# Routing the last layer's experts: compacted blocks of rows for three batches, dense for the fourth

## The reference, cut to what matters

```python
gate_probs = softmax(xf @ gate_w.T)                     # xf: 1024 tokens x 128
topk_scores, topk_idx = top_k(gate_probs, 2)            # 2 of 8 experts for each token
topk_scores /= sum(topk_scores)
combine = zeros((1024, 8)).at[token, topk_idx].set(topk_scores)
h = relu(einsum('td,ehd->teh', xf, w1) + b1)            # hidden 512, all 8 experts
expert_out = einsum('teh,edh->ted', h, w2) + b2
x = x + einsum('ted,te->td', expert_out, combine)
```

## Time and profile before

| | |
|---|---|
| Median of 3 runs | 380.56 us (379.95 to 383.03) |
| The profiled execution | 382.81 us |
| its span, first to last instruction | 381.0 us |
| PE, DVE, ACT, POOL busy | 314.1, 285.3, 233.0, 131.0 us |
| Mean granted PE clock | 0.900 of full |

### The profile page before, as it was taken

How to read it: one execution, slowest core, us unless ns; L and a number is a source line. 1 busy time by engine, 2 the same in 40 slices (tenths; PEclk the granted TensorE clock), 3 DMA queues, 4 the chain that set the end, 5 groups by cost and what they waited for, 6 DMA issues and landing times.

```text
span 381.0 us, 8587 instructions
## 1 busy us (share of the span) xinstructions
PE 314.1 (82%) x3064; PEld 208.3 (55%) x3064; DVE 285.3 (75%) x741; ACT 233.0 (61%) x380; POOL 131.0 (34%) x209
## 2 busy tenths in 40 slices
PE   0667639997879995797888878878999999999993
PEld 0452314564549974573564545545447676767773
DVE  5687502597987886777968999999997888765663
ACT  1257926776666542323147576756969997768981
POOL 4935897652033451407715032053122203000000
PEclk9999855899999995666558999999989999999999
DMA  7930000000000650000000000000000000010001
GB/s 217 382 150 1 2 0 3 2 2 1 2 2 0 224 223 0 0 3 0 0 2 2 1 2 3 2 3 2 0 2 3 3 2 2 2 29 0 3 3 29
DMA packets 4330, 12.39 MB, mean 33 GB/s; under 512 B 632, under 2 KB 2944, under 8 KB 3264
## 3 DMA queue, kind: packets, MB, share of 16 engines
q1 hardware_dynamic: 4288, 11.84, 8.5%
HBM read 11.31 MB, written 0.52 MB: 31 GB/s over the span
## 4 chain that ended last, share of the span: by engine, by line
PE 28%; DVE 19%; issue 4%; ACT 2%; POOL 0%; DVEq 0%; ACTq 0%; POOLq 0%
PE single L1563 11%; PE double L1550 10%; DVE mx L1053 6%; PE single L1236 2%; PE single L1229 1%; DVE mxc L1040 1%; DVE w L1184 1%; ACT hid L865 1%; DVE xn L933 1%; PE double L1416 1%; DVE y L998 1%; DVE qcn L1063 1%; PE double L1436 1%; DVE sums L992 1%; DVE tmp L1132 1%
## 5 line engine op out<-in xcount | busy, mean ns | idle before, releaser
L788 ACT ACTIVATE region_p<-double 128x1024 f32<-128x1024 f32 x64 | 64.3, 1025 | 23.5 <-PE double L1269 10.8
L688 POOL TENSOR_SCALAR_AFFINE_SELECT region_p<-region_p 128x512 f32<-128x512 f32 (+1 forms) x48 | 39.8, 830 | 58.5 <-ACT region_p L788 57.1
L1202 DVE TENSOR_TENSOR tmp<-hid,tmp 128x1024 f16<-128x1024 f32 x32 | 39.2, 1226 | 20.7 <-ACT tmp L874 20.4
L865 ACT ACTIVATE hid<-double,b1s 128x512 f32<-128x512 f32 x64 | 40.3, 680 | 12.3 <-PE double L1550 10.4
L1563 PE MATMUL single<-w,tmp 128*128 128x128 f16 x768 | 45.5, 219 | 2.2 <-issue 2.2
L1563 PEld LDWEIGHTS single<-w,tmp 128*128 128x128 f16 x768 | 43.9, 98 | 5.6 <-issue 2.9
L1550 PE MATMUL double<-xnT,w 128*128 128x512 f16 x168 | 40.5, 384 | 1.0 <-ACT hid L865 1.0
L646 POOL TENSOR_SCALAR rstd<-mv 128x2 f32<-128x2 f32 x24 | 6.2, 257 | 86.2 <-DVE mv L926 85.5
L874 ACT ACTIVATE tmp<-hid 128x1024 f16<-128x1024 f32 x32 | 33.8, 1057 | 1.6
L1053 DVE TENSOR_REDUCE mx<-double 128x4 f32<-128x1024 f32 (+1 forms) x24 | 29.4, 1225 | 1.5 <-PE double L1436 0.6
L1325 PE MATMUL outs<-region_p,vst 128*32 128x256 f32 x256 | 23.7, 450 | 6.5 <-POOL region_p L688 6.4
(11 more groups left out here) (279 smaller groups left out, 666.3 us busy)
## 6 DMA issues: line engine op xcount, KB each, us to landing
w<-in_w1a SPq DMA_DIRECT2D x2, 1024.0 KB, 11.8
w<-in_w2a SPq DMA_DIRECT2D x2, 1024.0 KB, 13.9
w<-in_w1b SPq DMA_DIRECT2D x2, 1024.0 KB, 4.9
w<-in_w2b SPq DMA_DIRECT2D x2, 1024.0 KB, 7.5
wb<-in_wb SPq DMA_DIRECT2D x1, 837.0 KB, 7.9
row<-in_row SPq DMA_DIRECT2D x1, 800.0 KB, 6.4
x<-in_x SPq DMA_DIRECT2D x4, 128.0 KB, 2.4
out<-x SPq DMA_DIRECT2D x4, 128.0 KB, 1.9
```

Of the source, the lines that this page charges most:

```text
L688: then(g.affine_select(out=v, in_=v, compare_op=ALU.is_ge, fill=0.0, base=0, pattern=[[0, n], [1, P]], channel_multiplier=-1), "prob_masked")
L788: a.activation(probs[:, slot("prob", key), :], psum(step), ACT.Exp, scale=SCALE).then_inc(psum_done[PSUM.slot(step)], 1)
L865: a.activation(hid0[:, slot("hid0", (h, e, n)), cols], psum(step)[:, cols], ACT.Relu, bias=b1s[:, c:c + 1]).then_inc(psum_done[PSUM.slot(s ...
L1202: then(v.tensor_tensor(hid[:, 1].rearrange("p c n -> p (c n)"), hid0[:, slot("hid0", (h, e, n)), :], hid[:, 0].rearrange("p c n -> p (c n) ...
```

## The change

For batches 0, 2 and 1 (`SPARSE`) each token's row is written twice to a buffer `moved` in device memory, at the next free row of each of its two experts. Blocks of 128 rows are then read back, one expert works on a block, and its output is stored over the block's rows. The first 128 rows of each expert are 8 fixed blocks; rows beyond that are 11 blocks whose expert and place come from a table that DVE makes (`tab`) and SP reads into registers. All 19 blocks are always executed. Finally each token's two result rows are fetched and added with their weights. Batch 3 (`LAST`) runs through all 8 experts densely. All products are plain fp32: no splits, no `b1s`, `ws`, `w2s`, `xs`, `hs`. The whole list of steps is a new one, also for work that does not change.

New steps: `rk` (PE counts the tokens of an expert ahead of each token; DVE makes row numbers), `sct` (POOL, 4 indirect writes of 128 rows for each batch), `tab` (10 small DVE operations), `xl` (SP reads a fixed block), `dl` (SP reads two registers, then an expert's weights, 514 KB, and a block), `bt` (transpose), `bu`, `bd` (up, down), `ys` (SP stores a block; for table blocks it reads a register first), `gat` (POOL, 4 indirect reads for each batch), `cb` (DVE sums).

```diff
+SPARSE = (0, 2, 1)
+LAST = 3
+ROOM = T * len(SPARSE)
+OVER = 11
+BLOCKS = NE + OVER
+ROWS = NE * ROOM + (OVER + 1) * P
+        "xl": NE, "wd": 3, "xbT": 2, "yb": 4}
...
 # SP, after the other loads, ahead of w1a and w2a
+            sp.wait_ge(sem("zeros_ready"), 1)
+            sp.dma_start(moved.rearrange("(n p) d -> p n d", p=P),
+                         yb[:, 0, :].unsqueeze(1).to_broadcast([P, ROWS // P, P]))
...
+            for step in ORDER:
+                if kind == "xl":
+                    sp.wait_ge(sem("scattered"), 16 * 4 * len(SPARSE))
+                    sp.dma_start(xl[:, slot("xl", n), :], moved[ROOM * n:ROOM * n + P, :])
+                elif kind == "dl":
+                    sp.wait_ge(sem("scattered"), 16 * 4 * len(SPARSE))
+                    sp.wait_ge(sem("table_ready"), 1)
+                    for b in range(NB):
+                        written(sp, ("ml", b, 3))
+                    read_by_tensor(sp, "xl", n)
+                    read_by_tensor(sp, "wd", n)
+                    of = sp.value_load(table[0:1, 1, i:i + 1], min_val=0, max_val=(NE - 1) * P)
+                    at = sp.value_load(table[0:1, 0, i:i + 1], min_val=0, max_val=ROWS - P)
+                    sp.dma_start(wd[:, slot("wd", n), :], d["experts"][bass.ds(of, P), :])
+                    sp.dma_start(xl[:, slot("xl", n), :], moved[bass.ds(at, P), :])
+                elif kind == "ys":
+                    written(sp, ("bd", n))
+                    if n < NE:
+                        dst = moved[ROOM * n:ROOM * n + P, :]
+                    else:
+                        at = sp.value_load(table[0:1, 0, n - NE:n - NE + 1], min_val=0, max_val=ROWS - P)
+                        dst = moved[bass.ds(at, P), :]
+                    sp.dma_start(dst, yb[:, slot("yb", n), :])
...
 # POOL
+                elif kind == "sct":
+                    for t in tiles_of(b):
+                        for k in range(2):
+                            g.indirect_dma_start(
+                                moved, bass.IndirectOffsetOnAxis(ap=spots[:, t, k:k + 1], axis=0),
+                                xn[:, 1, t, :], None).then_inc(sem("scattered"), 16)
+                elif kind == "gat":
+                    for n in range(BLOCKS):
+                        pool.wait_ge(sem(f"y_stored{s}"), 16 * (SLOTS["yb"].turn(n) + 1))
+                    for t in tiles_of(b):
+                        for k in range(2):
+                            g.indirect_dma_start(yg[:, t, k, :], None, moved,
+                                bass.IndirectOffsetOnAxis(ap=spots[:, t, k:k + 1], axis=0))
...
 # ACT
+                elif kind == "bt":
+                    evac(step, xbT[:, slot("xbT", b), :], psum(step)[:, 0:P])
+                elif kind == "bu":
+                    for c in range(HC):
+                        a.activation(hid[:, slot("hid", b), cols], psum(step)[:, cols], ACT.Relu, bias=bias1)
+                elif kind == "mup":
+                    for n in range(2):
+                        cols = slice(n * T, (n + 1) * T)
+                        a.activation(hid[:, slot("hid", (e, q)), cols], psum(step)[:, cols], ACT.Relu, ...)
...
 # DVE: bd is one 128x128 copy out of the accumulator; mdown two sums in place of four
+                elif kind == "cb":
+                    dve.wait_ge(sem(f"gathered{b}"), 16 * 4)
+                    for k in range(2):
+                        for t in tiles_of(b):
+                            ins = v.scalar_tensor_tensor(x[:, t, :], yg[:, t, k, :], gex[:, t, k:k + 1],
+                                                         x[:, t, :], ALU.mult, ALU.add)
...
 # PE
+                elif kind == "bu":            # w: a slice of w1, or of wd for a table block
+                    for c in range(HC):
+                        ins = mm(dst[:, c * P:(c + 1) * P], w[:, c * P:(c + 1) * P],
+                                 xbT[:, slot("xbT", b), :], start=True, stop=True)
+                elif kind == "bd":
+                    for c in range(HC):
+                        ins = mm(dst[:, 0:P], hid[:, slot("hid", b), c * P:(c + 1) * P], w, ...)
                 elif kind == "mup":           # batch 3 alone
+                    for n in range(2):
+                        ins = mm(dst[:, n * T:(n + 1) * T], w1[:, e, c * P:(c + 1) * P],
+                                 xnT[:, 1, toks(LAST)], start=True, stop=True)
                 elif kind == "mdown":
+                    for i in range(2):
+                        for c in range(HC):
+                            ins = mm(dst[:, i * P:(i + 1) * P], h, w2[:, e, c, :], ...)
...
 # the new list: layer 0, first kcx; layer 1, second kcx; from the gates to the end
+sc.0.3.0 kct.1 kcx.1 pv.0.1.3 q1.0 sc.0.3.1 pv.0.1.4 pv.0.1.5 oc.0.1 tr.1.2 sc.0.3.2 sc.0.3.3 ot.0.1
...
+ml.0.1 ml.2.0 ml.0.2 ml.0.3 lna.4.0 kct.4 p3a.3 lnb.4.0 p3b.3 ml.2.1 kcx.4 tr.4.0 k4.0 tr3.1 qc4.0
...
+rk.2 mxs.3.0 tr.6.1 sct.2 ga.1 gd.0 gb.1 mxs.3.1 rk.1 mxs.3.2 sct.1 mxs.3.3 xl.0 tq.5.3 xl.1 xl.2
...
+pv.4.3.3 sc.4.3.4 tqm.5.3 dl.8 dl.9 bt.8 bd.1 bd.2 bt.9 bu.8 dl.10 bd.0 ys.1 bu.9 bt.10 bd.8
+sc.4.3.5 bd.9 ys.8 bt.3 bu.10 sc.5.3.0 bu.3 pv.4.3.4 bt.5 pv.4.3.5 gc.1 pv.5.3.0 dl.11 ys.9 oc.4.3
+bd.10 ys.10 sc.5.3.1 dl.12 bt.11 dl.13 bu.5 ot.4.3 pv.5.3.1 oc.5.3 bu.11 bt.6 ot.5.3 bd.3 bd.11 ys.0
+bt.12 ys.3 ou.5.3 gd.1 ys.2 bu.6 bu.12 dl.14 op.5.3 lna.6.3 bd.5 bt.13 bd.12 bu.13 bt.7 lnb.6.3 bd.6
+tr.6.3 bt.14 ys.11 dl.15 ys.12 ys.6 bu.7 bu.14 ga.3 bd.13 gb.3 mup.0.0 ys.5 bd.14 ys.13 mup.0.1 gc.3
+bt.15 bd.7 bt.4 bu.15 gd.3 mup.1.0 dl.16 dl.17 bd.15 mdown.0 ys.14 bt.16 mup.1.1 dl.18 bu.16 bu.4
+mdown.1 bt.18 bd.16 bt.17 ys.15 ys.16 bu.18 bu.17 bd.4 mup.2.0 bd.17 bd.18 mup.2.1 ys.4 ys.17
+mup.3.0 mup.3.1 ys.18 mdown.2 mdown.3 mup.4.0 ys.7 gat.2 mup.4.1 mup.5.0 mup.5.1 mdown.4 mdown.5
+mup.6.0 mup.6.1 gat.0 mup.7.0 cb.0 mup.7.1 gat.1 cb.2 cb.1 mdown.6 mdown.7
```

More of the change, by code:

```diff
@@ L234, in the_steps @@
         hold("combT", b, ("gc", b), ("gd", b))
-    for e in range(NE):
[L236 to L243, removed]
-        for q in range(2):
[L245 to L252, removed]
+    add(("casts", 1), [], ("D", 0.3))
@@ new lines, in the_steps @@
+    for b in SPARSE:
+        add(("gat", b), [("ys", n) for n in range(BLOCKS)] + recurrent, ("G", 4.5), ("S", 0.0))
+        add(("cb", b), [("gat", b), ("gd", b)], ("D", 1.5))
+    for e in range(NE):
+        for q in range(2):
+            add(("mup", e, q), [("tr", 6, LAST)] + downs, ("P", 0.95), ("A", 0.9),
+                behind=[("mup", e, 0) if q else e and ("mup", e - 1, 1)])
+            hold("hid", (e, q), ("mup", e, q), ("mdown", e))
+        add(("mdown", e), [("mup", e, 0), ("mup", e, 1), ("gd", LAST)],
+            ("P", 1.85), ("D", 0.75), behind=[e and ("mdown", e - 1)])
@@ L306, in kind_of @@
         return f"ml{step[2]}"
-    staged = ("lna", "lnb", "tr", "sc", "pv", "oc", "ot", "ou", "op", "tq", "tqm", "mxc", "mxe")
+    staged = ("lna", "lnb", "tr", "sc", "pv", "oc", "ot", "ou", "op", "tq", "tqm", "mxc", "mxe", "casts")
     return f"{step[0]}{step[1]}" if step[0] in staged else step[0]
@@ L374 @@
[L374 to L396, removed]
-pv.4.2.4 pv.4.2.5 oc.4.2 sc.5.2.1 pv.5.2.0 ot.4.2 mxc.5.1.0 tqm.4.1 mxc.5.1.1 tk4.3 op.5.0 sc.4.1.0
@@ L1170, in _ @@
[L1170 to L1171 removed]
+                    first, second = gex[:, tiles(b), 0], gex[:, tiles(b), 1]
+                    full = [P, 2, 2, NE]
+                    iota = part(cst, CST, "iota").unsqueeze(1).unsqueeze(1).to_broadcast(full)
+                    then(v.tensor_tensor(hot[:, tiles(b), :, :], iota,
+                                         topf[:, tiles(b), :].unsqueeze(3).to_broadcast(full),
+                                         ALU.is_equal), wait=False)
@@ new lines, in _ @@
+                    then(v.tensor_scalar(first, second, 1.0, None, ALU.add))
+                    then(v.reciprocal(first, first))
+                    if b in SPARSE:
+                        then(v.tensor_tensor(hots[:, tiles(b), :], hot[:, tiles(b), 0, :],
+                                             hot[:, tiles(b), 1, :], ALU.add), "hots_ready", wait=False)
+                    then(v.tensor_tensor(second, second, first, ALU.mult))
+                    then(v.tensor_tensor(hotw[:, :, :, :], hot[:, tiles(b), :, :],
+                                         gex[:, tiles(b), :].unsqueeze(3).to_broadcast(full), ALU.mult))
```

405 lines of the change are left out of this document (247 added, 158 removed), and 5 rows, old and new, of the table LENGTHS.

## The result

The changed kernel takes 368.35 us (median of 4 runs, 367.19 to 369.14), the kernel before 380.25 beside it: ratio 0.968, 95% interval 0.963 to 0.974. It is faster, by 12 us where the forecast had 29.5; 368 lies inside the range, 17 us from the value. The range was drawn for dear or cheap transfers, which came near their forecast; that PE's work costs twice as much was not among its reasons, so the hit is owed to its width. The profiled execution took 368.68 us, its span 367.0.

The account below looks back on a forecast made before the run. PE's expert matmuls were taken to bound the last 100 us; afterwards a transfer chain would: `rk.1` 272.5, last store 329.8, last read landed 346.2, span end 351.3, median 351 us against 380.25 measured before; range 333 to 378.

Parts of the forecast that it names:

- fp32's price: PE, expert products: a plain fp32 matmul of 128 columns costs 0.115 us, from 3.81 us for 32 in layer 0.
- 35 us replace 92: PE, expert work: 19 blocks at 1.05 us and 15 us for dense batch 3 replace 91.7 us of matmuls.
- no engine can bound the tail: Last 100 us, bound by PE before: no engine bounds them after the change; the chain of transfers can.
- SP's waits, 4 us: SP's queue of `dl` and `ys`: stores ahead of loads wait for `bd` and PE's list, 4 us atop 43.6.
- The rest of the chain: From `rk.1` at 272.5 through scatter, `xl`, `dl`, `ys` (last store 329.8) and twelve reads at 1.05 to span end 351.3.
- Up to the first maximum: Stretch to layer 1's first row maximum: +4, -3 and +1.4 us make it 2.4 us earlier.
- the wait at `kcx`: Layer 0, near 41 us: PE waits 6.44 us for a mask behind POOL's `kcx`; moving `kcx.1` later gains 4 us.
- the second `kcx`: POOL, 11.67 us at 174.6, hidden before: now ahead of `lna.4.2`, it costs 3 us, between 0 and 6.
- From there to `rk.1`: First maximum to the last rank, on DVE: work added and removed nets +1.2 us; `rk.1` ends at 272.5.
- Dear register loads: Rival, SP's 33 loads between 282 and 330 cost more than 0.7 us each: 381 at 1.6, 390 at 1.9; chance 0.13.
- Dear indirect transfers: Rival, POOL's 16 indirect transfers on the path: 366 us at 2 us each, 381 at 2.9; chance 0.12.
- Cheap transfers with ACT at the end: Rival: loads at 0.3 and indirects at 0.7 us; ACT and dense batch 3 set the end, 335 us; chance 0.15.

Follow-up runs that it names:

- both_two_passes: Changed kernel with the expert products of blocks and dense batch each issued as two bf16 passes instead of fp32: 362.88 us, ratio 0.951 to the kernel before.
- pool_stores_ahead_two_passes: Changed kernel with expert products in two bf16 passes, block stores on POOL, five weight and eight result slots, each `dl` right behind its slot's release: 357.01 us, ratio 0.940.

## Why the prediction was wrong in size and right in sign

**fp32's price: the failed step.** "0.115 us each with the tail taken off" divides by its count of 32. That count is of records. `fup` issues 2 x 4 matmuls for each step, and the row spans two steps: 16 matmuls, 0.23 us each. From it come "35 us replace 92" (64 do) and "no engine can bound the tail". The row and the printed code together would have shown it. The Trainium skill (FP8 and Floating Point Precision, section TensorE Precision Notes) states that a true fp32 product takes four passes through the PE array. This case agrees: 0.223 us for 128 columns against 45.5/768 = 0.059 for fp16 in the earlier trace rows, 3.8 times. With 64 us for the experts PE is a bound of its own: it is busy 80 us from 280 on and ends at 361.

**SP's waits, 4 us: too small at any price of PE.** They are 17 in the changed kernel (19 with the table) and 10 in both_two_passes, where PE costs what the forecast assumed. The step took stores as waiting for PE's place in the list, once; the runs show a loop of load, landing, block and store through two in-order queues with three weight and four result slots. Price and loop are worth 5.5 and 5.9 us, in that order (by the ratios 1.7% and 1.1%), and the second only after the first.

**The rest of the chain held.** `dl` 2.45 for 2.4; `rk.1` 2.8 early; ReLU 0.28 for 0.27 (128 columns). `tab` was left out: its ten small operations stand behind two maxima on DVE, and SP waits 2.1 us for them before the first `dl`. The reads cost 1.25 for 1.05, 2.3 us, and the first waits 2.65 for the store to land, not 1.9. In pool_stores_ahead_two_passes, with the price near the forecast's and the loop untied, the time is 357 for 351. Of these 6 us the last store has 2.0, the landing 0.7, the reads 2.3, and the step from span to median 1.4, with 0.3 less at the very end.

**Up to the first maximum** 7.5 us came in (177.2 to 169.7) for the forecast's 2.4: the feed-forward's 4.3 for 4, though the wait at `kcx` that was to bring it hardly shrank, and the 3 us charged for the second `kcx` did not come. That is 5.1 us beside the forecast, past the 5 us that it had set as a sign of being wrong. (The first maximum is one of cross attention now; self-attention's starts at 171.0.) From there to `rk.1` it took 100.0 for 97.7, 2.3 more, so `rk.1` came 2.8 early.

**The rivals.** Dear register loads: no, 0.70. Dear indirect transfers: at 1.25 a little, also beside busy DVE, where scatters took 0.96 to 1.25 each. The lockout by DVE copies that the Trainium skill (SBUF - State Buffer, Who interferes with whom) describes was not put to the test: beside the scatters DVE ran row maxima out of the accumulators and short operations, no long copies, and no run here shows it. Cheap transfers with ACT at the end: ACT is busy 48 of 81 us from 280 to 361, no bound. No rival had PE as the bound, which is what came.

## What to carry to other kernels

Before a duration is divided by a count in a profile, the count is held against the code: one fp32 matmul here is two records and takes 3.8 times as long as an fp16 one. When loads and stores of one loop share an in-order queue, its length can be a round trip through the engines, not the sum of its issues; here slots, queue and engine had to be relieved together to see all of it. And work that only fills an engine's waits, like the dense batch here, may be what keeps its clock up.
